# Edge columns of a convolution on GpSimd, and an out projection from rounded halves, in a Mamba block between two feed-forward layers

## The reference, cut to what matters

```
gate, hbc, dt = split(x @ in_proj_w)              # 4096, 4096 + 2*128, 64 columns
hbc = silu(causal_conv_of_4_taps(hbc) + conv_b)   # each channel along the rows
xc, B, C = split(hbc);  dt = softplus(dt + dt_bias);  cum = cumsum(-exp(A_log) * dt) in a chunk
Y_diag = (C B' * decay * dt) @ xc                 # inside a chunk
state  = chunk_decay * state + B' @ (xc * dt * to_end)
Y_off  = (C @ state before the chunk) * exp(cum)
hidden = (Y_diag + Y_off + D * xc) * silu(gate)
out    = (rms_norm(hidden) * norm_w) @ out_proj_w # 4096 -> 256
```

## Time and profile before

| | us |
|---|---|
| median of 3 runs (range) | 1543.37 (1541.32 to 1545.97) |
| the profiled execution, its own time | 1541.9 |
| its span, first to last instruction | 1540.2 |
| PE busy in the span | 1390.8 (90%) |
| DVE | 1228.8 (80%) |
| ACT | 1040.0 (68%) |
| POOL | 651.8 (42%) |

### The profile page before, as it was taken

The page is one execution under the profiler, slowest core; times in us unless marked ns, Lnnn a source line. Parts: engine busy times, 40 slices in busy tenths (PEclk is TensorE's granted clock), DMA queues, the critical chain, the costliest instruction groups (busy, mean ns, idle before and its releaser), DMA issues. The chain is left out here.

```text
span 1540.2 us, 26251 instructions
## 1 busy us (share of the span) xinstructions
PE 1390.8 (90%) x8704; PEld 1083.1 (70%) x8704; DVE 1228.8 (80%) x2739; ACT 1040.0 (68%) x2133; POOL 651.8 (42%) x469
## 2 busy tenths in 40 slices
...
GB/s 122 69 89 21 15 14 28 63 47 96 118 110 103 116 102 100 90 120 109 104 115 105 102 90 112 111 106 116 103 106 90 106 111 108 96 96 178 12 16 27
DMA packets 102080, 136.37 MB, mean 89 GB/s; under 512 B 27744, under 2 KB 49856, under 8 KB 101824
## 3 DMA queue, kind: packets, MB, share of 16 engines
...
## 5 line engine op out<-in xcount | busy, mean ns | idle before, releaser
L836 ACT ACTIVATE M<-cum_row,cum_table 128x128 f32<-128x128 f32 x1024 | 311.9, 389 | 0.0
L968 POOL TENSOR_TENSOR xend<-xdt,to_end_table 128x512 f32<-128x512 f32 x128 | 142.0, 1109 | 367.8 <-DVE xdt L1186 367.7
L1175 DVE SCALAR_TENSOR_TENSOR xs<-psum,conv_w_sb,xs 128x511 f32<-128x511 f32 (+2 forms) x384 | 283.4, 738 | 5.0 <-ACT xs L850 4.9
L974 POOL TENSOR_TENSOR hid<-hid,sg 128x512 f32<-128x512 f32 x128 | 270.6, 2114 | 0.4 <-DVE hid L1231 0.4
L1563 PE MATMUL psum<-hid,wo 128*128 128x512 f32 x512 | 243.2, 597 | 9.7 <-ACT eT L747 9.4
L960 POOL TENSOR_TENSOR squares<-squares,sq 128x512 f32<-128x512 f32 x124 | 158.8, 1281 | 143.5 <-ACT sq L813 142.8
L1196 DVE TENSOR_TENSOR M<-M,CB 128x1024 f32<-128x1024 f32 x128 | 179.7, 1404 | 0.0
L1563 PEld LDWEIGHTS psum<-hid,wo 128*128 128x128 f32 x512 | 96.3, 190 | 84.5 <-issue 73.0
L813 ACT ACTIVATE sq<-hid 128x512 f32<-128x512 f32 x124 | 77.7, 626 | 114.7 <-POOL hid L974 114.7
L1523 PE MATMUL psum<-xend,B_tok 128*128 128x128 f32 x1024 | 138.3, 278 | 13.8 <-POOL xend L968 13.4
L1223 DVE TENSOR_TENSOR psum<-psum,e_row 128x512 f32<-128x512 f32 x128 | 89.5, 699 | 67.0 <-PE psum L1537 56.7
...
## 6 DMA issues: line engine op xcount, KB each, us to landing
cum_row<-cum_scratch SPq DMA_DIRECT2D x256, 256.0 KB, 4.4
e_row<-e_scratch SPq DMA_DIRECT2D x256, 128.0 KB, 3.6
...
```

The lines of the kernel that those rows point to most:

```text
L836: last = nc.scalar.activation(M[:, v % 3, h, c * CH:(c + 1) * CH], cum_row[:, v % 2, h, c * CH:(c + 1) * CH], ACT.Relu, bias=scalar_of(CUM ...
L968: nc.gpsimd.tensor_tensor(xend[:, v % 2], xdt[:, v % 3], per_chunk_head(TO_END, v), ALU.mult).then_inc(xend_done, 1)
L974: nc.gpsimd.tensor_tensor(hid[:, v % 2, :], hid[:, v % 2, :], sg[:, v % 8, :], ALU.mult).then_inc(hid_done, 1)
L1175: nc.vector.scalar_tensor_tensor(xs[:, v % 8, shift:], psum[:, X_BANK + v % 2, 0:TT - shift], tap_of(v, tap), xs[:, v % 8, shift:], ALU.mu ...
```

## The change

The out projection is made from halves. ACT scales `wo_raw` in place and rounds it to `wo_hi`, and POOL makes `wo_lo`; for each step ACT rounds the gated `hid` to `hid_hi` (`hid_to_hi`, ahead of `square`) and POOL subtracts it to `hid_lo` (`hid_to_lo`, ahead of `add_squares`), which lies in the place of `hid` and so waits for the square. `out_proj` waits for both halves and issues six fp32r matmuls in place of two float32 ones.

The edge columns are summed for four pairs at once by `sum_halos` on POOL, at s divisible by four where the tile of s+8 isn't the first, between `to_chunk_end` and `gate`: five products and sums of up to 12 columns, a copy and a last sum. `conv_tap` then has one edge instruction of three columns on DVE, which reads PSUM and `halo_sum`; it copies its own last columns first, and its taps run in the other order.

`xend` and `e_row` have one buffer in place of two, so `load_e` is issued one iteration later, behind `scale_off` of the step before. `gw_raw` has half its size, and the second half of the gate weights is loaded at u = 7 and split at u = 9. There is no zero state: for t = 0 the first scan is a copy, `off` leaves the first chunk out and `scale_off` its columns. In the ticks ahead of the loop, `wo` is split at k = 5, 6, 12 and 15 and the gate weights at 4 and 7. Left out of the diff below are names of semaphores, the count in `scans` and the order of allocations.

```diff
...
-    e_row = sb("e_row", [P, 2, TT], F32)
+    e_row = sb("e_row", [P, TT], F32)
...
-    xend = sb("xend", [P, 2, CPT, 2, HP], F32)
+    xend = sb("xend", [P, CPT, 2, HP], F32)
...
-    hid = sb("hid", [P, 2, TT], F32)
+    hid_hi = sb("hid_hi", [P, 2, TT], F32R)
+    under, sbu = scope()
+    hid = sbu("hid", [P, 2, TT], F32)
+    under.close()
+    hid_lo = sb("hid_lo", [P, 2, TT], F32R)
...
-    zero_state = sb("zero_state", [P, 2, HP], F32)
...
+    halo_prod = sb("halo_prod", [P, TAPS - 1, GP, TAPS - 1], F32)
+    halo_sum = sb("halo_sum", [P, 2, GP, TAPS - 1], F32)
...
 def load_g_weights(q):
...
-    if q >= 2:
-        sp.wait_ge(gw_lo_done, q - 1)
-    else:
-        sp.wait_ge(w_small_lo, 2)
-    at = q % 2 * half
-    sp.dma_start(gw_raw[:, :, at:at + half], w_in_t[:, :, q * half:(q + 1) * half]).then_inc(gw_in[q % 2], 16)
+    if q >= 1:
+        sp.wait_ge(gw_lo_done, q)
+    sp.dma_start(gw_raw[:], w_in_t[:, :, q * half:(q + 1) * half]).then_inc(gw_in, 16)
 def load_wo(p):
...
-        sp.wait_ge(wo_done, p - 1)
+        sp.wait_ge(wo_lo_done, p - 1)
...
 def load_e(v):
...
-    sp.wait_ge(off_scaled, nth(v - 2))
+    sp.wait_ge(off_scaled, nth(v - 1))
     for h in range(2):
-        sp.dma_start(e_row[h * HP:(h + 1) * HP, v % 2, :],
+        sp.dma_start(e_row[h * HP:(h + 1) * HP, :],
...
-                     .rearrange("p o t -> p (o t)")).then_inc(e_in[v % 2], 16)
+                     .rearrange("p o t -> p (o t)")).then_inc(e_in, 16)
...
-load_g_weights(1)
...
-store_x1(0)
+load_g_weights(1)
...
+store_x1(0)
...
-    if alive(s + 4):
-        load_e(s + 4)
+    if alive(s + 3):
+        load_e(s + 3)
...
+    if u == 7:
...
-    if u in (13, 14):
-        load_wo((g + 1) * GP + u - 11)
+    if u in (14, 15):
+        load_wo((g + 1) * GP + u - 12)
...
 def split_g_hi(q):
...
-    act.wait_ge(gw_in[q % 2], (q // 2 + 1) * 16)
+    act.wait_ge(gw_in, (q + 1) * 16)
...
-    nc.scalar.activation(gw_hi[:, :, cols], gw_raw[:, :, cols], ACT.Copy).then_inc(gw_hi_done, 1)
+    nc.scalar.activation(gw_hi[:, :, cols], gw_raw[:], ACT.Copy).then_inc(gw_hi_done, 1)
 def scale_wo(p):
...
-    else:
+        act.wait_ge(w_small_lo, 2)
+    nc.scalar.activation(wo_raw[:, p % 2, :], wo_raw[:, p % 2, :], ACT.Copy,
+                         scale=norm_sb[:, p:p + 1]).then_inc(wo_done, 1)
+    if p >= GP:
...
-    nc.scalar.activation(wo[:, p % GP, :], wo_raw[:, p % 2, :], ACT.Copy,
-                         scale=norm_sb[:, p:p + 1]).then_inc(wo_done, 1)
+    act.wait_ge(wo_done, p + 1)
+    nc.scalar.activation(wo_hi[:, p % GP, :], wo_raw[:, p % 2, :], ACT.Copy).then_inc(wo_hi_done, 1)
+
+def hid_to_hi(v):
+    act.wait_ge(hid_done, nth(v))
+    act.wait_ge(out_done, nth(v - 2))
+    nc.scalar.activation(hid_hi[:, v % 2, :], hid[:, v % 2, :], ACT.Copy).then_inc(hid_hi_done, 1)
...
     if alive(s):
+        hid_to_hi(s)
...
-    if g < GROUPS - 1 and u in (6, 8):
-        split_g_hi(2 * (g + 1) + u // 2 - 3)
+    if g < GROUPS - 1 and u in (6, 9):
+        split_g_hi(2 * (g + 1) + u // 3 - 2)
...
 def split_g_lo(q):
...
-    nc.gpsimd.tensor_tensor(gw_lo[:, :, cols], gw_raw[:, :, cols], gw_hi[:, :, cols].bitcast(F32),
+    nc.gpsimd.tensor_tensor(gw_lo[:, :, cols], gw_raw[:], gw_hi[:, :, cols].bitcast(F32),
...
+
+def sum_halos(v):
+
+    t, pairs, n = v // GP % NT, slice(pair_of(v), pair_of(v) + GP), sums_before(v)
+    pool.wait_ge(halo_in, GP * n)
+    pool.wait_ge(conv_done, nth(v - 5))
+    for tap in range(TAPS - 1):
+        w_tap = conv_w_sb[:, pairs, tap:tap + 1].to_broadcast([P, GP, TAPS - 1 - tap])
+        nc.gpsimd.tensor_tensor(halo_prod[:, tap, :, 0:TAPS - 1 - tap], halo[:, t % 2, :, tap:], w_tap,
+                                ALU.mult).then_inc(halo_step, 1)
+    pool.wait_ge(halo_step, 5 * n - 2)
+    nc.gpsimd.tensor_tensor(halo_prod[:, 1, :, 0:1], halo_prod[:, 1, :, 0:1], halo_prod[:, 2, :, 0:1],
+                            ALU.add).then_inc(halo_step, 1)
+    bias = conv_b_sb[:, pairs].unsqueeze(2).to_broadcast([P, GP, TAPS - 1])
+    nc.gpsimd.tensor_tensor(halo_prod[:, 0], halo_prod[:, 0], bias, ALU.add).then_inc(halo_step, 1)
+    pool.wait_ge(halo_step, 5 * n)
+    nc.gpsimd.tensor_copy(halo_sum[:, t % 2, :, 2], halo_prod[:, 0, :, 2])
+    nc.gpsimd.tensor_tensor(halo_sum[:, t % 2, :, 0:2], halo_prod[:, 0, :, 0:2], halo_prod[:, 1, :, 0:2],
+                            ALU.add).then_inc(halo_done, 1)
+
+def split_wo_lo(p):
+    pool.wait_ge(wo_hi_done, p + 1)
+    if p >= GP:
+        pool.wait_ge(out_done, nth(last_of(p - GP)))
+    nc.gpsimd.tensor_tensor(wo_lo[:, p % GP, :], wo_raw[:, p % 2, :], wo_hi[:, p % GP, :].bitcast(F32),
+                            ALU.subtract).then_inc(wo_lo_done, 1)
+
+def hid_to_lo(v):
+    pool.wait_ge(hid_hi_done, nth(v))
+    pool.wait_ge(sq_done, nth(v))
+    nc.gpsimd.tensor_tensor(hid_lo[:, v % 2, :], hid[:, v % 2, :], hid_hi[:, v % 2, :].bitcast(F32),
+                            ALU.subtract).then_inc(hid_lo_done, 1)
...
 def to_chunk_end(v):
...
-    pool.wait_ge(states_done, nth(v - 2))
+    pool.wait_ge(states_done, nth(v - 1))
...
-    nc.gpsimd.tensor_tensor(xend[:, v % 2], xdt[:, v % 3], per_chunk_head(TO_END, v),
+    nc.gpsimd.tensor_tensor(xend[:], xdt[:, v % 3], per_chunk_head(TO_END, v),
...
-    elif k - 1 < GP + 2:
-        split_g_lo(k - 1 - GP)
+    elif k - 1 in G_TICKS:
+        split_g_lo(G_TICKS.index(k - 1))
+    elif k - 1 in WO_TICKS:
+        split_wo_lo(WO_TICKS.index(k - 1))
...
     if alive(s):
+        hid_to_lo(s)
...
+    if s % GP == 0 and alive(s + 8) and (s + 8) % SLOTS >= GP:
+        sum_halos(s + 8)
...
+    if g > 0 and u == 0:
+        split_wo_lo(g * GP + GP - 1)
...
-    if u in (6, 8):
-        split_g_lo(2 * (g + 1) + u // 2 - 3)
+    if u in (6, 9):
+        split_g_lo(2 * (g + 1) + u // 3 - 2)
...
+    if u >= 13:
+        split_wo_lo((g + 1) * GP + u - 13)
...
 def conv_tap(v, step):
...
-    tap = TAPS - 2 - step
-    shift = TAPS - 1 - tap
+    shift = TAPS - 1 - step
...
+        if t < NT - 1:
+            nc.vector.tensor_copy(halo[:, (t + 1) % 2, j, :],
+                                  psum[:, X_BANK + v % 2, TT - TAPS + 1:TT]).then_inc(halo_in, 1)
+        if t > 0:
+            dve.wait_ge(halo_done, sums_before(v))
+            nc.vector.scalar_tensor_tensor(xs[:, v % 8, 0:shift], psum[:, X_BANK + v % 2, 0:shift],
+                                           tap_of(v, TAPS - 1), halo_sum[:, t % 2, j, :], ALU.mult, ALU.add)
...
-    if t > 0:
-        nc.vector.scalar_tensor_tensor(xs[:, v % 8, 0:shift], halo[:, t % 2, j, TAPS - 1 - shift:], tap_of(v, tap),
-                                       xs[:, v % 8, 0:shift], ALU.mult, ALU.add)
-    if tap == 0 and t < NT - 1:
-        nc.vector.tensor_copy(halo[:, (t + 1) % 2, j, :], psum[:, X_BANK + v % 2, TT - TAPS + 1:TT])
-    nc.vector.scalar_tensor_tensor(xs[:, v % 8, shift:], psum[:, X_BANK + v % 2, 0:TT - shift], tap_of(v, tap),
+    nc.vector.scalar_tensor_tensor(xs[:, v % 8, shift:], psum[:, X_BANK + v % 2, 0:TT - shift], tap_of(v, step),
...
-                                       conv_done if tap == 0 else conv_step, 1)
+                                       conv_done if step == TAPS - 2 else conv_step, 1)
...
+    if chunk == 0:
+        nc.vector.tensor_copy(inner[:, v % 2, 0].rearrange("p h q -> p (h q)"),
+                              psum[:, ST_BANK, 0:P]).then_inc(scan_step, 1)
+        return
...
-            before = zero_state[:, h, :] if t == 0 else carry[:, t % 2, j, h, :]
+            before = carry[:, t % 2, j, h, :]
...
 def scale_off(v):
...
-    dve.wait_ge(e_in[v % 2], (v // 2 + 1) * 32)
-    nc.vector.tensor_tensor(bank(Y_BANK), bank(Y_BANK), e_row[:, v % 2, :], ALU.mult).then_inc(off_scaled, 1)
+    dve.wait_ge(e_in, (v + 1) * 32)
+    cols = slice(CH if at_slot(v)[1] == 0 else 0, TT)
+    nc.vector.tensor_tensor(psum[:, Y_BANK, cols], psum[:, Y_BANK, cols], e_row[:, cols],
+                            ALU.mult).then_inc(off_scaled, 1)
 def skip_path(v):
...
-    dve.wait_ge(sq_done, nth(v - 2))
...
-                                xend[:, v % 2, c].rearrange("p h q -> p (h q)"), start=True, stop=True)
+                                xend[:, c].rearrange("p h q -> p (h q)"), start=True, stop=True)
...
 def off(v):
...
-    for c in range(CPT):
-        if c > 0:
-            before = inner[:, v % 2, c - 1]
-        else:
-            before = zero_state[:] if t == 0 else carry[:, t % 2, j]
+    first = 1 if t == 0 else 0
+    for c in range(first, CPT):
+        before = inner[:, v % 2, c - 1] if c > 0 else carry[:, t % 2, j]
...
-                                start=(c == 0), stop=False, skip_group_check=True)
+                                start=(c == first), stop=False, skip_group_check=True)
...
 def out_proj(v):
...
-    pe.wait_ge(hid_done, nth(v))
-    pe.wait_ge(wo_done, pair_of(v) + 1)
+    pe.wait_ge(hid_hi_done, nth(v))
+    pe.wait_ge(hid_lo_done, nth(v))
+    pe.wait_ge(wo_lo_done, pair_of(v) + 1)
...
```

(44 more changed lines are left out.)

5 lines of the change are left out of this document (2 added, 3 removed).

## The result

| | before | after |
|---|---|---|
| median of 4 runs each (range), us | 1542.53 (1541.32 to 1545.97) | 1589.49 (1588.13 to 1593.28) |
| ratio, 95% interval | | 1.0304 (1.0286 to 1.0322) |
| span of the profiled execution | 1540.2 | 1591.5 |
| mean granted clock of PE | 0.971 | 0.938 |

The change makes the kernel 47 us slower; 19 were forecast. What the page of after shows of this is little: PE's mean granted clock is lower, but in the loop only one digit of its clock line is 8 where the line of before has 9. One digit is a fortieth of the span, so short losses hardly show.

The account below looks back on a forecast made before the run. No one engine was taken to bound the kernel: PE waits, and DVE's list is as long or longer. The profiled 1541.9 us, plus 13 for seven groups and 7 for the last steps, gave 1562 us; range 1549 to 1575.

Parts of the forecast that it names:

- What bounds before: Main loop before: no one engine explains 135.6 us a group; PE alone could go faster, DVE's list is as long or longer.
- DVE and the edges: DVE's `conv_tap`: three edge instructions of 474 ns become one of 0.14 us plus a 0.06 copy; `scale_off` to `skip_path` 5.30 to 4.90.
- a sign of being wrong: Listed signs against the forecast: groups of 124 or 133, `sum_halos` over 5 us, DVE waiting for `e_row` or `halo_sum`.
- The new wait: Behind the long ACT iteration, `out_proj(s+1)` waits for rounding, square and POOL's difference; groups become 136.8 to 138.0 us, seven groups +13.
- T: The end of `gate(s)` on POOL, s divisible by four, from which the forecast counts its times.
- M's hold: DVE's instruction M, just ahead of POOL's difference, holds POOL 1.1 us, putting `out_proj(s+1)` at T + 15.8.
- So PE waits 2.1 us: PE ahead of `out_proj(s+1)` behind the long ACT iteration: ready at T + 13.0, but unable to begin before T + 15.1.
- The last steps: Steps 115 to 127, without projections: 0.6 x 7 for POOL's longer list and 2.5 for the last step's longer way, 7 us.
- What costs nothing: Terms put at 0: later `e_row` loads, weight loads, the one `xend` buffer, the zero state's memset, ticks ahead of the loop.
- rival (c): GpSimd's small instructions or the `e_row` transfers are dearer: 20 to 45 us more, 1582 to 1607 us; chance 0.17.
- Rival (a): The same chain behind the long ACT iteration without the hold by M: groups of 133.4, 1534 us; chance 0.16.
- (b): In the loop, `hid_lo` never ends last and PE sets the pace: groups of 123.3, 1463 us; chance 0.08.

Follow-up runs that it names:

- experiment 4: Two halves alone: the kernel before with only the edge sums on POOL, 1512.6 us; the changed kernel with before's edge instructions, 1626.1 us.
- the run with twelve products: The changed kernel with twelve unused products on PE ahead of `proj_x` in each iteration behind the long ACT iteration: 1568.1 us.
- experiment 3: The changed kernel with twelve unused PE products behind each long ACT iteration and eight ahead of `out_proj` in each of the last seven steps: 1564.4 us.
- experiment 7: The kernel of experiment 6 with `load_e(s+3)` issued ahead of `load_cum(s+5)` on SP in iterations with s % 4 == 0: 1530.8 us.
- experiment 6: The changed kernel with `hid_to_hi` and `square` of s+1 between `relus` and `exps`, and POOL's two weight splits behind the next `hid_to_lo` and `add_squares`: 1531.1 us.

## Why the prediction was right or wrong

The sign was right, the size wrong: +19 forecast, +47 measured, and 1589.5 lies just inside the range, whose top stood there for another reason.

**What bounds before.** Right. The edge instructions on DVE were worth what the argument said; with them gone and `out_proj` waiting for the gate alone, as before, a group takes 130.7 to 132.4 (experiment 4).

**DVE and the edges.** Right: 214 ns forecast as 0.14 to 0.2, no hold by POOL (223 ns at most of 96), as the rule of the Trainium skill (GPSIMD Engine Reference, 8. Key points) has it that was weighed in the forecast. `sum_halos` was taken as 1.8 us; the six that aren't held take 0.2 each, and the hold of the first makes it 2.3. DVE waited for `halo_sum`, 0.8 us at most, which the forecast had named as a sign of being wrong; the groups at full clock show no price of it.

**The new wait.** Right in place, cause and about in length: T + 16.0 against T + 15.8, an idle time of 2.05 to 3.92, 3.0 in the mean, against 2.8 (the 2.1 and the rest of M's hold), a mean of 34.1 for four steps against 34.0 to 34.3 where the clock stays full, groups of 136.7 against 136.8 to 138.0. M's hold, taken as 1.1, was 0.55 of `hid_lo`'s 1.83 in both periods shown. By the run with twelve products the groups cost 8 us at full clock, where 13 were taken; which of the terms make the rest was not taken apart.

**The step that failed** is the one from "So PE waits 2.1 us" to the period, "5.34 to `out_proj(s+2)`, 7.63 to `out_proj(s+3)`": the wait was priced as its own length, with the work behind it at the full rate, and the clock stood at nothing without a reason. `out_proj(s+1)` came when the forecast said, but `states(s+4)`, which it had at T + 18.2 to 18.5, began at T + 20.4 (712.60) behind the fall and at T + 18.4 (854.05) where there was none. Each such wait can be followed by 3.4 or 6.8 us at half clock, in which `out_proj`, `off` and `states` take 5.9 us instead of 3.2. PE was busy 129.7 of 135.6 us before, so little is there to hide that. It happened behind 19 of the 29 waits, 18 of them in the seven groups, where it cost 29 us, more than the whole forecast. I read the clock of one steady group and took it as a constant, though the edit was to put idle time into just this engine. The Trainium skill (TensorE: Matmul & The Clock Gate, HAM oscillation — how this bites in real kernels) describes a kernel whose PE falls to the lower clock again and again behind its waits; this trace agrees, with 22 stretches in the loop, but the waits here are for another engine and not for a transfer.

**The last steps.** +7 forecast, +12.6 measured. The term that was mis-sized is 0.6 us a step for POOL's list, taken as 5.8 us of work "with half of the growth hidden". POOL's step is 7.05, because the wait of 1.32 for ACT's round and square lies inside the list, right behind the gate. Clock is about 1 us of it (experiment 3). The starts of `out_proj` divide the rest: from step 121 to 126 there were 25.6 us before (1368.88 to 1394.52) and 33.3 after (1409.34 to 1442.62), 1.5 more a step and 7.6 in all. The last step's longer way was taken as 2.5 and measured 2.8, and 0.8 more in its products at half clock; 1.4 lie ahead of step 121.

**What costs nothing.** Right for `e_row` (experiment 7 shows it even where it waits) and, as far as the groups at full clock can tell, for the small instructions; the shorter `off` was not measured by itself. So rival (c), which ends at the measured time, is not what happened: it put 20 to 45 us on small sums and landings, and here `halo_sum` was waited for 13.4 us in all, 0.8 at most at a time, and `scale_off`, by the tile `e_row`, never for a transfer: those of the long iteration shown were issued at 703.3, as forecast 11.1 behind T, and landed 4.7 to 5.0 us later, not 5.4 to 7.2. Rival (a), the chain without M's hold, and (b), PE's pace, didn't occur in this kernel; experiment 6 comes near (a)'s groups, 132.6 against its 133.4, by another road, with the rounding and the square moved ahead of `exps`.
